# Graph and feed-forward block on one core: where the degrees' column is turned, and when the identity's read is asked for

## The chip, the core and the metric

The kernel runs on one core of a Trainium2 chip. The metric is the device time of one execution in microseconds (us); lower is better. Three executions of the kernel before took 1198.85, 1199.94 and 1200.19 us, a median of 1199.94 us.

## The reference

`x` has 1250 nodes of 1024 features; 20000 edges run from `src` to `dst`. Cut to what matters here:

```python
xn  = layernorm(x)
deg = segment_sum(ones, dst);  deg_inv = 1 / maximum(deg, 1)
def sage(h, Ws, Wn, b):
    mean = segment_sum(h[src], dst) * deg_inv[:, None]
    return h @ Ws + mean @ Wn + b
gnn = sage(relu(sage(xn, Ws0, Wn0, b0)), Ws1, Wn1, b1)
mix = gelu(V(xn @ Wq, xn @ Wk, xn @ Wv) @ Wo + bo)   # linear attention, feature by feature
x   = x + gnn + mix
out = x + ffn(layernorm(x))       # products of quantised codes
```

All the products are made from pairs of f16 parts (a high and a low one), so each product of two f32 matrices is three f16 matmuls.

## The kernel before, in words

Each engine has one program, written out by hand; engines meet at semaphores (`wait_ge`, `then_inc`), and nothing reorders an engine's work. SP (SyncE) asks for nearly all transfers, in the order in which they are written; ACT asks for two at the start.

**Start.** DVE writes `diagonal`, a [128 x 129] tile whose first column is 1. ACT sends it to device memory (L640, semaphore `diag_out`), waits for that (L641), and reads it back with rows of 128 instead of 129, which gives the identity `ident32` (L642, semaphore `ident_in`). PE waits for `ident_in` (L935) before its first transpose. Meanwhile SP asks for ten row tiles of `x` (125 nodes each, `x_all`, L450 to L455) and, between tiles 4 and 5, for the first two slices of weights, of `Wq` and `Wk` (`load(0)`, `load(1)`); behind tile 9 come the edge lists, two more slices (`Wv`, `Ws0`), the biases, and from L479 on the edge keys, which wait for DVE. For each tile DVE makes mean and variance (`x_stats`, L1194), ACT the normed rows (`xn_tile`, L653), PE eight transposes into PSUM (`turn_xn`, L947), ACT the high f16 part (`turned_hi`, L660), DVE the low one (`turned_lo`, L1251). In ACT's own order (L744 to L774) the squares of the two slices of weights (`norms(0, ...)`, L670) and the roots for tiles 2 to 4 (`deviations(1)`, L647) stand ahead of `turned_hi(0)`.

**Products on x.** PE multiplies the normed rows by Wq, Wk, Wv and Ws0 (L970, L983), group of 128 features by group, then by Wo and by Wn0, in halves of 512 columns and tiles of 125 rows (`half_product`, L1053), 40 tiles counted by `i` (0 to 39). `P16` takes the products by Wn0, through ACT (`p_high`, L822) and DVE (`p_low`, L1483). Tile i uses PSUM bank (i + 5) % 6; `mm_free` counts the tiles that DVE has read. GpSimd counts the edges into a matrix of 1250 x 1250 in device memory (L598), which becomes `AT` in f16 (`counts`, L1280).

**Degrees.** Behind tiles 35 and 37 PE sums the columns of `AT` (`degrees`, L991) into banks 6 and 7. DVE takes them behind its own parts of tiles 36 and 38 (L1491 to L1497): maximum with 1 (L1321), and after the second part the reciprocal of 128 x 1250 values (L1497), which sets `dinv_ok`. Only then comes `p_low(39)`. `dinvb` has all nodes' 1/degree in every partition's row.

**Turning the degrees.** For the second aggregation, 1/degree is also wanted as a column per tile of nodes (`dcol`). PE waits for `dinv_ok` (L1071) and makes ten one-row transposes into bank 6 (L1073, `dcol_done`). DVE waits for `dcol_done` (L1507), copies the column (L1508), makes a factor (L1509, L1510) and multiplies `dinvb` by it (L1512).

**First aggregation.** `for g in range(KC)` (L1076) runs over eight groups of 128 features: 60 matmuls each (L1085), of `P16` by `AT`, into PSUM banks 3 to 5 for even g, 0 to 2 for odd g. Groups 0 and 1 wait for `mm_free` to reach 37 and 40, later ones for `ag_free`, DVE's word that the group two before has been read. DVE per group: multiply by `dinvb` (L1524, sets `ag_free`), add the self product (L1527), after ACT's relu (L831) the low part (`h_low`, L1516). Behind it PE goes on to the halves 4 to 7 on `hT` (L1053, L1089 to L1092).

**The rest.** The second aggregation (L1114, L1123) has eight transposes of the next stage between its tiles (L1101); then the feed-forward products (L1151, L1181) and the output.

Of the kernel before, what the change touches and what calls it, by code (L numbers as in the profile page):

```python
# [38 lines left out]
def build(nc, x, src, dst, Ws0, Wn0, b0, Ws1, Wn1, b1, Wq, bq, Wk, bk, Wv, bv, Wo, bo, wgate, wup, wdown, out):  # L39
# [4 lines left out]
    NT = 10  # L44
    TP = N // NT
# [30 lines left out]
    with ctx:  # L76
# [15 lines left out]
        def sb(name, shape, dt, offset=None):  # L92
            if offset is None:
                offset = region(size(shape, dt))
            return nc.alloc_sbuf_tensor_at(name, shape, dt, offset=offset)
# [51 lines left out]
        dinvb = sb("dinvb", [P, N], F32, RG)  # L147
# [27 lines left out]
        ident32 = const("ident32", [P, P], F32)  # L175
# [43 lines left out]
        def bank(b, n=1):  # L219
            return ps[:, b * 512:(b + n) * 512]  # L220

        def acc(par):
            return ps[:, par * 1536:par * 1536 + 1536]
# [7 lines left out]
        def sem(name):  # L231
            return ctx.enter_context(nc.semaphore(name))
# [15 lines left out]
        diag_set, diag_out, ident_in = sem("diag_set"), sem("diag_out"), sem("ident_in")  # L248
# [6 lines left out]
        deg_done, deg_free, dinv_ok, dcol_done = (  # L255
            sem(n) for n in ("deg_done", "deg_free", "dinv_ok", "dcol_done"))
# [92 lines left out]
        for i in range(40, 80):  # L349
            n, t = divmod(i, NT)  # L350
# [29 lines left out]
        def ag1_banks(t, h, n=1):  # L380

            return bank(2 * ((t + 1) % 3) + h, n)
# [4 lines left out]
        def last_bank(n):  # L387
            a, b = LAST_COLS[n]
            return (ag1_banks(NT - 1, n) if n < 2 else ag1_banks(NT - 3, 0))[:, 0:b - a]
# [11 lines left out]
        def w9(j, *of):  # L401

            return w_last[:, of[0], of[1]] if j == NF - 1 else w8[:, j, of[0], of[1]]
# [4 lines left out]
        def load_rows(sp, tile, of, t, done):  # L408

            if t + 1 < NT:  # L410
                sp.dma_start(tile[:, t, :], of[t * TP:t * TP + P, :]).then_inc(done, 32)
            else:
                sp.dma_start(tile[:SPLIT, t, :], of[t * TP:t * TP + SPLIT, :]).then_inc(done, 16)
                sp.dma_start(tile[SPLIT:TP, t, :], of[t * TP + SPLIT:(t + 1) * TP, :]).then_inc(done, 16)
# [7 lines left out]
        def rows(t):  # L422
            return slice(t * TP, (t + 1) * TP)
# [4 lines left out]
        def _(sp):  # L428
            def load(r):

                if r >= NR:
                    worked(sp, r - NR)
                kind, *of = ring[r]
                slot = raw[:, r % NR, :]
                if kind == "chunk":
                    g, i = of
                    view = XW[i].rearrange("(k p) n -> p k n", p=P)[:, :, bass.ts(g, P)]
                    sp.dma_start(slot.rearrange("p (k n) -> p k n", k=KC), view).then_inc(raw_in[r % NR], 16)
                elif kind == "norm":
                    w, k = of  # L440
                    sp.dma_start(slot, MW[w][k * P:(k + 1) * P, :]).then_inc(raw_in[r % NR], 16)
                elif kind == "half":
                    w, h, j = of
                    view = MW[w].rearrange("(k p) n -> p k n", p=P)[:, 2 * j:2 * j + 2, h * HD:(h + 1) * HD]
                    sp.dma_start(slot.rearrange("p (k n) -> p k n", k=2), view).then_inc(raw_in[r % NR], 16)
                else:
                    sp.dma_start(slot.rearrange("p (k n) -> p k n", k=KC), ffn_chunk(of[0])).then_inc(
                        raw_in[r % NR], 16)

            for t in range(5):  # L450
                load_rows(sp, x_all, x, t, x_in[t])
            load(0)
            load(1)
# [480 lines left out]
        def _(pe):  # L934
# [78 lines left out]
            for h in range(2):  # L1013
                mm = pe.transpose(bank(2)[:EP, h * EH:(h + 1) * EH], key_r[:, h, :], ident32[:EH, :EH])
# [12 lines left out]
            for c in range(2, 4 * KC):  # L1027
                product(c)
                g, i = divmod(c, 4)
# [5 lines left out]
            def half_product(n, stationary):  # L1035
                w, part = HALVES[n]
                for t in range(NT):
                    i = 10 * n + t
                    if n == 0 and t < 6:
                        pe.wait_ge(xn_free[0 if (i + 5) % 6 < 3 else 1], 2 * KC)  # L1040
                    elif n == 4 and t < 6:
                        pe.wait_ge(ag_free[0 if t >= 3 else 1], KC // 2)
                    else:
                        pe.wait_ge(mm_free, i - 5)
                    for k in range(KC):
                        if n == 0 and t == 0:
                            pe.wait_ge(v_lo, k + 1)
                        elif n == 4 and t == 0:
                            pe.wait_ge(hl_ok, k + 1)
                        if t == 0 and k % 2 == 0:  # L1050
                            worked(pe, at["half", w, part, k // 2])
                        for ap, wp in ((0, 0), (0, 1), (1, 0)):
                            mm = pe.matmul(half_bank(i), stationary[:, k, ap, t * TP:t * TP + P],  # L1053
                                           hb[:, n % 2, k, wp, :], start=(k == 0 and wp == 0 and ap == 0),
                                           stop=(k == KC - 1 and ap == 1))
                    mm.then_inc(mm_done, 1)
                    if i in W_SUMS:
                        w_sums(W_SUMS[i])
                    if i == DEG_TILE - 1:
                        pe.wait_ge(so_ok, WN1 + 1)  # L1060
                        pe.wait_ge(at_ok, NT + 1)
                        degrees(0, 1024)
                    elif i == DEG_TILE + 1:
                        pe.wait_ge(deg_free, 1)
                        degrees(1024, N)
# [2 lines left out]
            half_product(1, VT)  # L1068
            half_product(2, xnT)
            half_product(3, xnT)  # L1070
            pe.wait_ge(dinv_ok, 1)  # L1071
            for t in range(NT):
                mm = pe.transpose(bank(6)[:TP, t:t + 1], dinvb[0:1, rows(t)], ident32[0:1, 0:1])  # L1073
            mm.then_inc(dcol_done, 1)

            for g in range(KC):  # L1076
                par = (g + 1) % 2
                if g < 2:
                    pe.wait_ge(mm_free, 37 + 3 * g)
                else:  # L1080
                    pe.wait_ge(ag_free[par], g // 2)
                for s in range(NT):
                    for part in range(2):
                        for a, b in NCOLS:
                            mm = pe.matmul(acc(par)[:, a:b], P16[:TP, s, part, bass.ts(g, P)], AT[:TP, s, a:b],  # L1085
                                           start=(s == 0 and part == 0), stop=(s == NT - 1 and part == 1))
                mm.then_inc(ag_done, 1)

            half_product(4, hT)  # L1089
            half_product(5, hT)  # L1090
# [14 lines left out]
            for t in range(NT):  # L1105
# [4 lines left out]
                if t + 1 < NT:  # L1110
                    for h in range(2):
                        for s in range(NT):
                            for part in range(2):
                                mm = pe.matmul(ag1_banks(t, h), AT[:TP, s, t * TP:t * TP + P],  # L1114
                                               P16[:TP, s, part, h * HD:(h + 1) * HD],
                                               start=(s == 0 and part == 0), stop=(s == NT - 1 and part == 1))
                else:
                    for n, (a, b) in enumerate(LAST_COLS):
                        if n == 2:
                            pe.wait_ge(ag1_free, NT - 2)  # L1120
                        for s in range(NT):
                            for part in range(2):
                                mm = pe.matmul(last_bank(n), AT[:TP, s, t * TP:t * TP + P], P16[:TP, s, part, a:b],  # L1123
                                               start=(s == 0 and part == 0), stop=(s == NT - 1 and part == 1))
# [11 lines left out]
            for n, (m, r) in enumerate(UG):  # L1136
# [7 lines left out]
                for b in range(IC):  # L1144
                    if r == 0:
                        pe.wait_ge(w9_in[IC + IC * m + b], 16)
                    for k in range(KC):
                        if n == 0 and b == 0 and k % (KC // 2) == 0:
                            pe.wait_ge(c_lo, k // (KC // 2) + 1)
                        for wp, ap in ((0, 0), (0, 1), (1, 0)):  # L1150
                            mm = pe.matmul(acc(n % 2)[:, b * 512:b * 512 + hi - lo],  # L1151
                                           w9(IC + IC * m + b, wp, slice(k * P, (k + 1) * P)),
                                           codeT[:, k, ap, lo:hi], start=(k == 0 and wp == 0 and ap == 0),
                                           stop=(k == KC - 1 and wp == 1))
# [13 lines left out]
            for r, (a, b) in enumerate(OCOLS):  # L1168
                if r > 0:
                    pe.wait_ge(o_lo, OFIRST + r)  # L1170
                for t in range(a // TP, b // TP):
                    wide = P if b == N or (t + 1) * TP < b else TP
                    for c in range(2):
# [3 lines left out]
                        for k in range(IC):  # L1177
                            if i == 0 and k < OFIRST:
                                pe.wait_ge(o_lo, k + 1)
                            for ap, wp in ((0, 0), (0, 1), (1, 0)):  # L1180
                                mm = pe.matmul(bank(i % 6)[:wide, :], o16[:, k, ap, t * TP:t * TP + wide],  # L1181
                                               w9(k, wp, slice(c * HD, (c + 1) * HD)),
                                               start=(k == 0 and wp == 0 and ap == 0),
                                               stop=(k == IC - 1 and ap == 1))
# [572 lines left out]
```

## Time and profile of the kernel before

| What | Value |
|---|---|
| Median of 3 executions | 1199.94 us |
| Profiled execution, its own time | 1197.6 us |
| Span of its instructions | 1195.8 us |
| Mean granted TensorE clock | 0.996 of 2.4 GHz |
| PE matmul, busy | 1154.0 us (97% of the span) |
| DVE, busy | 670.2 us (56%) |
| ACT, busy | 356.4 us (30%) |
| DMA, mean | 98 GB/s |

The span runs from the first to the last instruction; 1.8 us of the execution lie around it. PE is TensorE's matmuls, PEld its loads of stationary data, DVE VectorE, ACT ScalarE, POOL GpSimd, SP SyncE; a name with a q (SPq) is that engine's queue of requests. "Idle before" is the time in which an engine stood still just ahead of an instruction, with what released it behind the arrow. In the chain of waits each piece is what held up the next piece, so its pieces add up to the span.

### The profile page before, as it was taken

To read this page: it belongs to the slowest core of one execution; us is meant where nothing else is said; L and a number is where in the kernel's file an instruction comes from. 1 tells how busy PE (TensorE), PEld (TensorE's weight loads), DVE (VectorE), ACT (ScalarE), POOL (GpSimd) and SP (SyncE) were. 2 spreads that over 40 slices of the span, in tenths; PEclk is the share of its full clock that TensorE was granted. 3 is DMA by queue.
4 is the path that set the end of the run, shared out by engine and by line. 5 is a ranking of instruction groups with operands and counts; after the bars stand their busy time and mean duration, and the time that the engine had idled before them with its cause. 6 is when DMAs were issued, how large, how long until landed. Compare 5 with 4: busy or idle time off the path is not lost.

```text
span 1195.8 us, 15245 instructions
## 1 busy us (share of the span) xinstructions
PE 1154.0 (97%) x6309; PEld 621.8 (52%) x6309; DVE 670.2 (56%) x1232; ACT 356.4 (30%) x446; POOL 393.2 (33%) x224
## 2 busy tenths in 40 slices
PE   4899999999999999999999899999999999999978
PEld 3455555555555554444444455444444445579934
DVE  7766846749476663334433445646473335582663
ACT  5635243242333422323311022313110012252540
POOL 1266776868778774777300000000000000000000
PEclk9999999999999999999999999999999999999989
DMA  9935526254352439434711134332320070000005
GB/s 261 339 87 154 113 43 153 20 136 77 79 111 20 98 67 332 113 54 139 262 43 39 61 117 149 113 100 88 106 71 36 18 158 1 1 1 2 1 12 160
DMA packets 156151, 117.61 MB, mean 98 GB/s; under 512 B 93401, under 2 KB 132569, under 8 KB 155058
## 3 DMA queue, kind: packets, MB, share of 16 engines
q1 hardware_dynamic: 86744, 103.41, 27.6%
q0 software_dynamic: 69024, 13.07, 8.4%
q8 instruction: 49, 0.80, 0.3%
q10 hardware_dynamic: 314, 0.16, 0.0%
q14 instruction: 20, 0.16, 0.0%
HBM read 90.13 MB, written 21.41 MB: 93 GB/s over the span
## 4 chain that ended last, share of the span: by engine, by line
PE 92%; DVE 4%; issue 1%; ACT 1%; DMA 1%; SPq 0%; POOL 0%; POOLq 0%; ACTq 0%
PE ps L1053 34%; PE ps L983 32%; PE ps L1085 7%; PE ps L1114 6%; PE ps L1151 6%; PE ps L1181 3%; PE ps L970 1%; DMA raw<-in_L_mix_Wk_dram 1%; PE ps L1123 1%; DVE dinvb L1497 1%; PE ps L1101 1%; DVE key_b L1263 0%; PE ps L991 0%; DVE stats L1197 0%; ACT xs L653 0%
## 5 line engine op out<-in xcount | busy, mean ns | idle before, releaser
L598 POOL DMA_INDIRECT at_scratch<-copies,cell x160 | 345.6, 2160 | 161.1 <-DMA at_scratch<-copies,cell 89.1
L983 PE MATMUL ps<-xnT,whl 128*128 128x512 f16 (+1 forms) x2160 | 381.8, 339 | 0.0
L983 PEld LDWEIGHTS ps<-xnT,whl 128*128 128x128 f16 x2160 | 210.6, 98 | 168.9
L1053 PE MATMUL ps<-hb,hT 128*128 128x512 f16 x960 | 207.7, 379 | 1.3 <-DVE hT L1516 1.3
L1053 PEld LDWEIGHTS ps<-hb,hT 128*128 128x128 f16 x960 | 94.0, 98 | 114.4 <-DVE hT L1516 1.8
L579 POOL PARTITION_ALL_REDUCE ag_fw<-am_fw x9 | 3.2, 354 | 312.7 <-DVE am_fw L1399 312.7
L1053 PE MATMUL ps<-hb,VT 128*128 128x512 f16 x480 | 103.9, 379 | 1.5 <-ACT S_b L740 1.5
L1053 PE MATMUL ps<-hb,xnT 128*128 128x512 f16 x480 | 104.2, 379 | 0.0
L1085 PE MATMUL ps<-AT,P 125*128 125x512 f16 (+1 forms) x480 | 86.1, 343 | 0.0
L1114 PE MATMUL ps<-P,AT 125*128 125x512 f16 x360 | 79.0, 379 | 0.0
L1483 DVE SCALAR_TENSOR_TENSOR P<-ps,P 125x512 f16<-125x512 f32 x40 | 27.5, 689 | 91.9 <-ACT P L822 91.8
L1053 PEld LDWEIGHTS ps<-hb,VT 128*128 128x128 f16 x480 | 46.9, 98 | 58.0 <-ACT S_b L740 1.9
L1053 PEld LDWEIGHTS ps<-hb,xnT 128*128 128x128 f16 x480 | 47.0, 98 | 56.1
L575 POOL PARTITION_ALL_REDUCE ag<-am x5 | 1.8, 351 | 218.3 <-DVE am L1610 218.3
L1151 PE MATMUL ps<-codeT,w 128*128 128x250 f16 x600 | 65.2, 269 | 2.1 <-DVE codeT L1636 2.1
L1085 PEld LDWEIGHTS ps<-AT,P 125*128 125x128 f16 x480 | 47.1, 99 | 38.6 <-issue 1.6
L1151 PEld LDWEIGHTS ps<-codeT,w 128*128 128x128 f16 x600 | 57.8, 96 | 8.9 <-issue 1.8
L822 ACT ACTIVATE P<-ps 125x512 f16<-125x512 f32 x40 | 23.7, 594 | 116.4 <-PE ps L1053 116.3
L1114 PEld LDWEIGHTS ps<-P,AT 125*128 125x128 f16 x360 | 35.2, 98 | 40.9
L688 ACT ACTIVATE whl<-raw,sc 128x1024 f16<-128x1024 f32 x32 | 35.0, 1138 | 69.1 <-DVE inv L1233 69.1
L1245 DVE SCALAR_TENSOR_TENSOR whl<-raw,sc,whl 128x1024 f16<-128x1024 f32 x32 | 40.3, 1281 | 15.8 <-ACT whl L688 15.8
L1460 DVE SCALAR_TENSOR_TENSOR ps<-ps,sv,bo_b 125x512 f32<-125x512 f32 x20 | 15.0, 757 | 52.5 <-PE ps L1053 41.0
(231 smaller groups left out, 1204.6 us busy)
## 6 DMA issues: line engine op xcount, KB each, us to landing
raw<-in_L_gnn_W_neigh_dram SPq DMA_DIRECT2D x32, 512.0 KB, 4.5
raw<-in_L_gnn_W_self_dram SPq DMA_DIRECT2D x24, 512.0 KB, 5.2
key_b<-key_scratch SPq DMA_DIRECT2D x8, 1250.0 KB, 7.0
raw<-in_L_mix_Wo_dram SPq DMA_DIRECT2D x16, 512.0 KB, 3.6
parts<-at_scratch POOLq DMA_DIRECT2D x20, 312.5 KB, 4.7
at_scratch<-zeros POOLq DMA_DIRECT2D x6, 1020.0 KB, 17.8
x_all<-in_x_dram SPq DMA_DIRECT2D x9, 512.0 KB
x_acc<-in_x_dram SPq DMA_DIRECT2D x9, 512.0 KB
```

Source lines behind the costliest of these rows:

```text
L598: pool.indirect_dma_start(out=at_scr[c % 2][:, :], out_offset=bass.IndirectOffsetOnAxis(ap=cell[:, c:c + 1], axis=0), in_=copies[:, c:c + ...
L688: act.activation(whl[:, i, 0, :, :].rearrange("p k n -> p (k n)"), raw[:, at["chunk", g, i] % NR, :], ACT.Copy, scale=sc[:, g % 2, i:i + 1 ...
L822: act.activation(P16[:TP, t, 0, h * HD:(h + 1) * HD], half_bank(i)[:TP, :], ACT.Copy, scale=scale).then_inc(p_hi, 1)
L983: mm = pe.matmul(acc_of(c)[:, a:b], whl[:, i, wp, k, :], xnT[:, k, ap, a:b], start=(k == 0 and wp == 0 and ap == 0), stop=(k == KC - 1 and ...
L1053: mm = pe.matmul(half_bank(i), stationary[:, k, ap, t * TP:t * TP + P], hb[:, n % 2, k, wp, :], start=(k == 0 and wp == 0 and ap == 0), st ...
L1085: mm = pe.matmul(acc(par)[:, a:b], P16[:TP, s, part, bass.ts(g, P)], AT[:TP, s, a:b], start=(s == 0 and part == 0), stop=(s == NT - 1 and ...
L1114: mm = pe.matmul(ag1_banks(t, h), AT[:TP, s, t * TP:t * TP + P], P16[:TP, s, part, h * HD:(h + 1) * HD], start=(s == 0 and part == 0), sto ...
L1151: mm = pe.matmul(acc(n % 2)[:, b * 512:b * 512 + hi - lo], w9(IC + IC * m + b, wp, slice(k * P, (k + 1) * P)), codeT[:, k, ap, lo:hi], sta ...
L1181: mm = pe.matmul(bank(i % 6)[:wide, :], o16[:, k, ap, t * TP:t * TP + wide], w9(k, wp, slice(c * HD, (c + 1) * HD)), start=(k == 0 and wp ...
L1245: dve.scalar_tensor_tensor(whl[:, i, 1, :, :].rearrange("p k n -> p (k n)"), raw[:, at["chunk", g, i] % NR, :], sc[:, g % 2, i:i + 1], whl ...
L1460: dve.scalar_tensor_tensor(b, b, sv[:TP, INV_O:INV_O + 1], bo_b[:TP, h * HD:(h + 1) * HD], ALU.mult, ALU.add).then_inc(m1_ok, 1)
L1483: dve.scalar_tensor_tensor(P16[:TP, t, 1, at_p], half_bank(i)[:TP, :], scale, P16[:TP, t, 0, at_p], ALU.mult, ALU.subtract).then_inc(mm_fr ...
```

## The change

Two edits. SP waits for `diag_out` before it asks for tile 3 of `x`, so that ACT's read of the identity, which waits for the same semaphore, is not behind tiles 3 and 4 of `x` and the first weights. PE makes the ten transposes of the degrees (with the wait for `dinv_ok`) behind the matmuls of the aggregation's group 0 and no longer ahead of them. DVE's program is unchanged.

```diff
             for t in range(5):
+                if t == 3:
+
+                    sp.wait_ge(diag_out, 16)
                 load_rows(sp, x_all, x, t, x_in[t])
             load(0)
             load(1)
@@
             half_product(3, xnT)
-            pe.wait_ge(dinv_ok, 1)
-            for t in range(NT):
-                mm = pe.transpose(bank(6)[:TP, t:t + 1], dinvb[0:1, rows(t)], ident32[0:1, 0:1])
-            mm.then_inc(dcol_done, 1)
-
             for g in range(KC):
                 par = (g + 1) % 2
                 if g < 2:
@@
                 mm.then_inc(ag_done, 1)
+                if g == 0:
+                    pe.wait_ge(dinv_ok, 1)
+                    for t in range(NT):
+                        mm = pe.transpose(bank(6)[:TP, t:t + 1], dinvb[0:1, rows(t)], ident32[0:1, 0:1])
+                    mm.then_inc(dcol_done, 1)
```

## Rows read from the trace of the kernel before

**Rows 1.** The page: chain that ended last, shares of the span by line.

```profile
PE ps L1053 34%; PE ps L983 32%; PE ps L1085 7%; PE ps L1114 6%; PE ps L1151 6%; PE ps L1181 3%; PE ps L970 1%; DMA raw<-in_L_mix_Wk_dram 1%; PE ps L1123 1%; DVE dinvb L1497 1%; PE ps L1101 1%; DVE key_b L1263 0%; PE ps L991 0%; DVE stats L1197 0%; ACT xs L653 0%
```

**Rows 2.** Chain of waits, 640 to 765: start us, us, what.

```profile
648.14 5.20 PE ps L1053 x24
...
655.02 7.98 DVE dinvb L1497
...
663.04 1.53 PE ps L1073 x10
664.56 86.00 PE ps L1085 x480
```

**Rows 3.** Timeline, 630 to 775: start us, us, engine, line, operation [idle before].

```profile
642.66 0.69 DVE L1483 SCALAR_TENSOR_TENSOR P<-ps,P 125x512 f16<-125x512 f32 x1 [8.81 <-ACT P L822]
...
647.98 10.53 PE L1053 MATMUL ps<-hb,xnT 128*128 128x512 f16 x48
...
663.04 1.53 PE L1073 MATMUL ps<-ident,dinvb 1*125 1x1 f32 x10 [4.53 <-DVE dinvb L1497]
...
676.73 0.10 DVE L1522 MEMSET hT<- 128x48 uint32 x1 [10.43 <-PE ps L1085]
...
687.19 1.46 DVE L1524 TENSOR_TENSOR Tg<-ps,dinvb 128x1250 f32<-128x1250 f32 x1 [4.67 <-PE ps L1085]
...
697.76 1.46 DVE L1524 TENSOR_TENSOR Tg<-ps,dinvb 128x1250 f32<-128x1250 f32 x1 [4.78 <-PE ps L1085]
...
750.59 1.46 DVE L1524 TENSOR_TENSOR Tg<-ps,dinvb 128x1250 f32<-128x1250 f32 x1 [3.76 <-PE ps L1085]
```

**Rows 4.** Busy time by stretch, 653 to 677; PEclk is the granted clock.

```profile
653.30:658.50 5.20, 5.20 (x25) 2.16 (x22) 4.47 (x3) 0.60 (x1) 0.00 (x0) 1.00 0.00 0
664.50:666.00 1.50, 1.50 (x6) 0.63 (x6) 1.31 (x7) 0.00 (x0) 0.00 (x0) 0.50 0.00 0
666.00:668.00 2.00, 2.00 (x10) 0.96 (x9) 0.30 (x1) 0.00 (x0) 0.00 (x0) 0.68 0.00 0
668.00:670.00 2.00, 2.00 (x14) 1.05 (x12) 0.00 (x0) 0.00 (x0) 0.00 (x0) 1.00 0.00 0
```

**Rows 5.** Chain of waits, whole span: transposes between the second aggregation's tiles.

```profile
976.68 0.85 PE ps L1101 x8
977.54 8.63 PE ps L1114 x40
```

**Rows 6.** Timeline, 663 to 667: DVE behind the transposes.

```profile
662.90 0.63 DVE L1483 SCALAR_TENSOR_TENSOR P<-ps,P 125x512 f16<-125x512 f32 x1
...
664.79 0.16 DVE L1508 COPY dcol<-ps 125x10 f32<-125x10 f32 x1
...
665.43 0.87 DVE L1512 TENSOR_SCALAR dinvb<-dinvb,sv 128x1250 f32<-128x1250 f32 x1
```

**Rows 7.** Requests to landing in the first 40 us (last column: median us).

```profile
raw<-in_L_mix_Wk_dram SPq DMA_DIRECT2D x1, 512.0 KB, 10.2
diag_scratch<-diagonal ACTq DMA_DIRECT2D x1, 64.5 KB, 4.6
ident<-diag_scratch ACTq DMA_DIRECT2D x1, 64.0 KB, 4.9
```

**Rows 8.** Timeline, 0 to 40: the start.

```profile
5.77 0.33 ACTq L642 DMA_DIRECT2D ident<-diag_scratch  x1
...
10.75 3.59 PE L947 MATMUL ps<-ident,xs 125*128 125x125 f32 x16 [10.75 <-DMA ident<-diag_scratch]
...
14.08 1.06 ACT L670 ACTIVATE squared<-raw 128x1024 f16<-128x1024 f32 x1 [0.67 <-DMA raw<-in_L_mix_Wk_dram]
...
15.37 0.99 ACT L660 ACTIVATE xnT<-ps 128x1000 f16<-128x1000 f32 x1
```

**Rows 9.** Busy time by stretch, DMA: last two columns are share and GB/s.

```profile
0.00:6.70 6.70, 0.00 (x0) 0.00 (x0) 2.27 (x7) 0.57 (x1) 0.92 (x11) 1.00 0.70 244
0.73:1.73 1.00, 0.00 (x0) 0.00 (x0) 0.23 (x2) 0.00 (x0) 0.72 (x7) 1.00 0.00 0
3.30:9.00 5.70, 0.00 (x0) 0.00 (x0) 3.94 (x12) 1.59 (x3) 0.00 (x0) 1.00 1.04 408
```

**Rows 10.** Chain of waits, the start: from the weights' landing on.

```profile
2.12 0.04 issue
...
3.80 10.20 DMA raw<-in_L_mix_Wk_dram
...
52.62 9.84 PE ps L970 x72
```

## The prediction

> **What bounds the kernel now.** I read the page's chain first. The lines that hold it are PE's matmuls nearly throughout [rows 1]; two lines that are no matmul carry about one per cent each, the landing of the first slice of Wk and the reciprocal of the degrees, L1497. Those are the two places of the change. Time taken out of PE's line anywhere behind the start is therefore time taken off the end, unless something else comes to wait.
>
> Next the chain near the aggregation [rows 2]: PE's tile 38, then DVE's reciprocal for 7.98 us, the ten transposes for 1.53, then the 480 matmuls of the aggregation. The timeline shows how much of this PE really loses [rows 3]. Tile 39 runs beside the reciprocal and ends at 647.98 + 10.53 = 658.51; PE then stands still for 4.53 us until 663.04. The third view is the clock [rows 4]: 1.00 up to 658.5 (2.4 GHz); behind the stop 0.50 (1.2 GHz) from 664.5 to 666, 0.68 on average until 668, then 1.00 again. So group 0 of the aggregation pays for the stop a second time.
>
> At the start I read the chain again [rows 10]: it goes through Wk's landing at 14.0, then through ACT and DVE in turn, to PE's product at 52.6. The identity is not in it.
>
> **Part one: the transposes behind group 0.** Group 0 asks only for `mm_free` 37, that is DVE's part of tile 36, done at 642.66 + 0.69 = 643.35 [rows 3]. So it starts where tile 39 ends, at 658.51.
> - A group at full clock: from DVE's take-up of group 1 to that of group 2, 697.76 - 687.19 = 10.57; over the seven intervals from 676.73 to 750.59, 73.86 / 7 = 10.55 [rows 3]. Group 0 before, from 664.56 to 676.73 [rows 2, 3], took 12.17, so 1.62 more, the half clock.
> - Group 0 after: 658.51 + 10.55 = 669.06. The reciprocal is ready at 663, six us earlier, so PE doesn't wait for `dinv_ok`.
> - The transposes: 1.53 at half clock is the upper bound [rows 2]. The lower one is the eight transposes of the later stage at full clock, 0.85 us, or 0.106 each [rows 5]: ten take 1.06. I take 1.25, between the two, as these are of another shape. End: 670.31.
> - Seven more groups, 73.86: 744.17, against 750.59. Gain 6.4 us, which is 4.53 of stop, 1.62 of clock and 0.28 of faster transposes. Bounds 6.1 to 6.6 from the transposes alone.
>
> What waits now? DVE's work behind `dcol_done` runs from 664.79 to 665.43 + 0.87 = 666.30, so 1.5 us [rows 6]. It used to lie under group 0; now it stands between group 0's end and its reading. DVE is done with it at 671.8 and frees group 0's banks, after one more multiplication of 1.46 [rows 3], at 673.3. Group 2 wants them at 670.31 + 10.55 = 680.9. Cover 7.6 us, so cost 0; were it gone, each us more of DVE's work would cost one. Group 1 wants `mm_free` 40, given behind the reciprocal at 663.5 [rows 6]: there seven us early. From group 1 on, each wait has the distances it had before. The last thing PE waits for, the low part of group 7, moves with group 7.
>
> At the clock, the row shows that eight transposes of 0.85 us between two tiles of matmuls cost nothing beyond themselves, the 40 matmuls behind them taking 8.63 us as a full-speed piece [rows 5]. The Trainium skill, "TensorE: Matmul & The Clock Gate", section "Part 4: PE-mode transpose", says that a transpose does not count as busy the way a matmul does. By that rule the ten might act as a stop; the sum would lose up to the 1.62 us that a real stop has cost. I go by the row.
>
> **Part two: SP's wait at tile 3.** ACT's request for the identity leaves at 5.77, when `diag_out` is there [rows 8]; SP's wait ends at the same event. Up to then SP has asked for tiles 0 to 2 (the third request ends by 2.12 [rows 10]); so tile 3 is asked for at about 5.8 in place of 2.2, and tile 4, Wq and Wk follow, each later than before. Everything behind them on SP's queue, tiles 5 to 9, edges, weights, biases, is held too.
> - What hides it: the DMA engines work off a backlog at 408 GB/s [rows 9]. Three tiles (512 KB each, as Wk [rows 7]) and the diagonal are 1.64 MB; by 6.70 the core had moved 244 x 6.7 = 1.63 MB [rows 9]. So there is work until 6.7. Tile 3's first bytes come some 1.0 us after the request, as at the beginning (nothing moves from 0.73 to 1.73 [rows 9]), at 6.8. The hole is nominally 0.1 us, more if the rate takes time to rise, as it does at the start. The identity's 64 KB, 0.16 us at that rate, fall into it and leave Wk's way. Bounds: 0 (all covered) and 3.6 (Wk late by the whole pause). I take 0.4, near the covered end, because the backlog is in the rows.
> - What it brings: the identity, now landing 4.9 us after its request with much traffic ahead [rows 7], may land two us or so sooner. PE's first transposes would start before 10.75 by some tenths, as ACT's normed tile is there about then. But their reader, ACT at L660, starts at 15.37, behind the squares of Wk, which begin at 14.08 with its landing [rows 8]. The transposes end at 14.3, already before it. Gain 0.
> - Wk's delay passes on one to one, as the chain has no slack between 14.0 and 52.6 [rows 10].
>
> **Sum.** -6.4 + 0.4 = -6.0 us. The profiled execution's own 1197.6 becomes 1191.6. It lies 2.3 under the median of the three; on the median's scale, 1199.94 - 6.0 = 1193.9.
>
> **Rivals.**
> 1. *The pause at the start is not covered.* If `diag_out` or the refilling of the queue is slow, Wk lands up to 3.6 late: 1199.9 - 6.4 + 3.6 = 1197.1. For it: the rate rises slowly at the beginning, and Wk is in the chain [rows 10]. Against: the backlog until 6.7. Chance 0.12, counting a delay over 1.5.
> 2. *The clock falls in the transposes*: the ten count as a stop and group 1 begins at half clock, as group 0 did behind the real one, +1.62 [rows 2, 3], so 1195.5. Against: the transposes that left the next tile at full speed [rows 5]. Chance 0.05. This is what the rule of the Trainium skill named above would give.
> 3. *The start gets faster.* Wk lands sooner, because the identity's traffic and later tiles no longer mix into it, or PE's earlier transposes matter: up to 1 us, 1192.5. For it: PE's stop of 10.75 us is the longest named at the start [rows 8]. Against: ACT's order. Chance 0.15.
> 4. *Slower than before.* The place is again SP's wait: it costs one us for each us that `diag_out` comes behind about 5.7. The other part's gain is eaten from 5.7 + 6.4 = 12.1 on. The diagonal took 4.6 to land with more traffic beside it [rows 7]; with less it should not take 11. At 15, the time would be 1202.8. Chance 0.02.
> 5. *The move of the transposes brings nothing*, because PE waits elsewhere in the aggregation: only if DVE's extra 1.5 us met less than that of cover, and it has 7.6. Time 1200.3. Chance 0.04.
>
> The forecast itself, 1193 to 1195.4, has 0.62.
>
> **Numbers.** A measurement of this kernel tells 0.2% from no change, 2.4 us, so faster means below 1197.5. The forecast and rivals 2 and 3 are all faster, and nearly all of rival 1. Faster 0.91, same 0.06, slower 0.03. For eight in ten I reach from rival 3's end, less the spread of some tenths of a median (1198.85 to 1200.19 among three), to just under rival 1's end: 1191.8 to 1196.6.
>
> **What would show it.** In the changed kernel: no idle time of PE before L1085's first matmul, which starts about 658 plus what the start lost; L1073 behind it, with no wait for `dinv_ok`, taking 1.1 to 1.5 us; clock 1.00 throughout; the first DVE L1508 some 6 us later than before and L1524 at full pace, with no wait of PE for DVE at groups 2 to 7. At the start: tile 3 asked for at 5.8, the identity landing before 10, Wk at 14.0 to 15.0, and the product L970 at 52.6 to 53.6 still last. Wrong would be: Wk at 16 or later, a PE wait for `ag_free`, or a clock of 0.5 in group 1.

## The result

The changed kernel took 1192.75 us in the median of four executions (1192.35 to 1194.39), against 1199.70 before (four executions, 1198.85 to 1200.19). The ratio is 0.9945, 95% interval 0.993 to 0.996: 6.6 us faster by the ratio, between 4.8 and 8.4. Forecast were 1193.9, range 1191.8 to 1196.6. The profiled execution of after took 1193.08 (span 1191.3), that of before 1197.6: those two differ by 4.5 us only. That is 2 us less than the ratio says, and most of the experiments go to this difference.

The chain of waits of after, 635 to 765 us (start, us, what), beside [rows 2]:

```profile
649.88 10.36 PE ps L1056 x48
660.25 10.57 PE ps L1083 x60
670.81 1.18 PE ps L1089 x10
671.99 74.09 PE ps L1083 x420
```

The reciprocal has left the chain. Tiles 38 and 39 (10.36 us for both) are followed without a stop by group 0, in 10.57 us, then the transposes in 1.18, then seven groups in 74.09. The busy time by stretch has the clock (PEclk, third from the end) at 1.00 throughout, where [rows 4] fell to 0.50:

```profile
658.00:670.00 12.00, 12.00 (x67) 6.36 (x66) 8.34 (x10) 0.60 (x1) 0.00 (x0) 1.00 0.17 53
670.00:672.00 2.00, 2.00 (x16) 1.53 (x15) 0.00 (x0) 0.00 (x0) 0.00 (x0) 1.00 0.00 0
```

DVE in the timeline of after, beside [rows 6]: its work behind the transposes now begins at 672.03, and group 0 is read from 673.64 on. Group 1 is taken at its proper time, 682.70.

```profile
672.03 0.17 DVE L1511 COPY dcol<-ps 125x10 f32<-125x10 f32 x1 [5.41 <-PE ps L1089]
...
672.68 0.87 DVE L1515 TENSOR_SCALAR dinvb<-dinvb,sv 128x1250 f32<-128x1250 f32 x1
...
673.64 1.41 DVE L1527 TENSOR_TENSOR Tg<-ps,dinvb 128x1250 f32<-128x1250 f32 x1
...
682.70 1.46 DVE L1527 TENSOR_TENSOR Tg<-ps,dinvb 128x1250 f32<-128x1250 f32 x1 [3.32 <-PE ps L1083]
```

The start, in the timeline of after, beside [rows 8]:

```profile
5.54 0.36 ACTq L645 DMA_DIRECT2D ident<-diag_scratch  x1
...
6.86 0.58 SPq L438 DMA_DIRECT2D raw<-in_L_mix_Wk_dram  x1
...
10.81 3.60 PE L950 MATMUL ps<-ident,xs 125*128 125x125 f32 x16 [10.81 <-DMA ident<-diag_scratch]
...
15.86 1.06 ACT L673 ACTIVATE squared<-raw 128x1024 f16<-128x1024 f32 x1 [0.69 <-DMA raw<-in_L_mix_Wk_dram]
```

The squares of Wk begin 1.78 us later than before, and the identity is there no sooner: PE's first transposes start at 10.81 against 10.75. The DMA traffic by stretch (last two columns: share, GB/s) shows the hole, in this profile of after:

```profile
6.00:7.00 1.00, 0.00 (x0) 0.00 (x0) 0.93 (x5) 1.00 (x1) 0.00 (x0) 1.00 0.64 262
7.00:8.00 1.00, 0.00 (x0) 0.00 (x0) 0.93 (x4) 0.21 (x1) 0.00 (x0) 1.00 0.45 133
8.00:9.00 1.00, 0.00 (x0) 0.00 (x0) 0.66 (x5) 0.24 (x2) 0.00 (x0) 1.00 0.98 372
```

PE's product of 72 matmuls, the first piece of the chain behind the start, begins at 54.37 against 52.62 in [rows 10], 1.75 later. Shifted back by that, the aggregation ends 6.2 us sooner (746.08 - 1.75 = 744.33 against 664.56 + 86.00 = 750.56 [rows 2]): 4.53 of stop and 1.7 of clock. So the two profiles say: -6.2 + 1.75 = -4.5. Do they stand for the usual execution?

### The profile page after: what moved, and what is told of

It reads as the page before. It is cut to its first block, busy times and chain, and to the rows that moved or that the text cites. A ratio compares the mean times of both kernels' runs of the same rounds, so it can differ in the third digit from the quotient of the medians.

```text
span 1191.3 us, 15245 instructions
## 1 busy us (share of the span) xinstructions
PE 1155.2 (97%) x6309; PEld 622.5 (52%) x6309; DVE 669.0 (56%) x1232; ACT 356.3 (30%) x446; POOL 389.6 (33%) x224
## 4 chain that ended last, share of the span: by engine, by line
PE 94%; DVE 3%; issue 1%; DMA 1%; ACT 1%; SPq 0%; POOL 0%; POOLq 0%; ACTq 0%
PE ps L1056 34%; PE ps L986 32%; PE ps L1083 7%; PE ps L1117 7%; PE ps L1154 6%; PE ps L1184 3%; PE ps L973 2%; DMA raw<-in_L_mix_Wk_dram 1%; PE ps L1126 1%; PE ps L1104 1%; PE ps L994 0%; DVE stats L1200 0%; PE ps L950 0%; DVE xnT L1254 0%; DMA diag_scratch<-diagonal 0%
## 5 line engine op out<-in xcount | busy, mean ns | idle before, releaser
L601 POOL DMA_INDIRECT at_scratch<-copies,cell x160 | 341.9, 2137 | 164.5 <-DMA at_scratch<-copies,cell 95.6
```

Source lines behind the costliest of these rows:

```text
L601: pool.indirect_dma_start(out=at_scr[c % 2][:, :], out_offset=bass.IndirectOffsetOnAxis(ap=cell[:, c:c + 1], axis=0), in_=copies[:, c:c + ...
```

## The experiments

Each was run beside the kernel before on the same chip: runs 1 to 4 on one chip (median of before 1199.29), 5 to 8 on a second (1199.51), 9 to 11 on a third (1198.95). Where two experiments are compared, it is by their medians. "The wait" is SP's wait for `diag_out`, "the turning" the move of the ten transposes, and "the product of 72 matmuls" PE's first product behind the start, L970 of the kernel before. Line numbers in the profiles move by a few lines with each edit.

**1. Both edits.** 

> Both edits, as changed. The profiles of before and after differ by 4.5 us of span, the medians of the timed executions by 6.95. Theory 1 (the turning of the degrees gains 6.2 us, SP's wait costs 1.7 us by Wk's later landing): 4.5 us faster than before, ratio 0.9962. Theory 2 (SP's wait costs nothing, or gains, in a usual execution): 6.2 us faster or more, ratio 0.9948 or less.

Measured: 1192.12 us, ratio 0.9944 (0.993 to 0.9957), 7.2 under the 1199.29.

**2. SP's wait alone.**

```diff
             for t in range(5):
+                if t == 3:
+                    sp.wait_ge(diag_out, 16)
                 load_rows(sp, x_all, x, t, x_in[t])
```

> SP's wait ahead of tile 3 alone. Theory 1: 1.7 us slower than before, ratio 1.0014, Wk landing at 15.8 us. Theory 2: within 0.5 us of before, or faster. In both the aggregation is as before: PE stands still 4.5 us ahead of the ten transposes and group 0 takes 12.2 us.

Measured: 1199.69 us, ratio 1.0002 (0.9993 to 1.0011): 0.4 us slower in the median; the interval, 0.8 us faster to 1.3 slower, excludes 1.7. The squares of Wk begin at 14.89. The aggregation holds the surprise, in its chain of waits and its busy time by stretch:

```profile
655.76 7.98 DVE dinvb L1500
...
663.78 2.25 PE ps L1076 x10
666.04 86.28 PE ps L1088 x480
```

```profile
664.00:666.00 2.00, 2.00 (x11) 1.98 (x12) 1.34 (x9) 0.00 (x0) 0.00 (x0) 0.50 0.00 0
666.00:668.00 2.00, 2.00 (x7) 0.84 (x7) 1.42 (x4) 0.00 (x0) 0.00 (x0) 0.50 0.00 0
668.00:670.00 2.00, 2.00 (x10) 0.96 (x8) 0.00 (x0) 0.00 (x0) 0.00 (x0) 0.67 0.00 0
```

The stop is 4.53 us, as before, but what follows it is dearer: the transposes take 2.25 us in place of 1.53, and the clock is back at 1.00 only after 668, where in [rows 4] it was by then. This stretch of code is the same as in the kernel before. From tile 39's end at 659.25 to the end of the aggregation it takes 93.07 us, and 92.05 in the profile of before (658.51 to 750.56): the clock's part is 2.7 us here, in place of 1.7.

**3. The turning alone.** The second edit without the first.

> The ten transposes behind group 0 alone, no wait on SP. Theory 1: 6.2 us faster than before, ratio 0.9948, and 1.7 us faster than with both edits; Wk lands at 14.0 us. Theory 2: no faster than with both edits.

Measured: 1191.81 us, ratio 0.9937 (0.9924 to 0.9951), 7.5 under 1199.29 and 0.3 under both edits. Its chain has group 0 in 10.57 us, the transposes in 1.18 and seven groups in 74.09, as after. So by the medians the turning gains more than the 6.2 of the two profiles. This run's own interval, 5.9 to 9.1 us, does not exclude 6.2; that runs 6 and 10, which also have the turning without the wait, lie 7.7 and 7.2 under before speaks against it as well. The wait's 1.7 is excluded by run 2. Theory 1 falls in its sizes.

**4. SP's wait ahead of tile 1.** Both edits, `t == 3` made `t == 1`.

> Both edits, but SP waits ahead of tile 1, so only tile 0 is asked for before the diagonal has landed. Theory 1 (the wait costs what it leaves the DMA engines without work): two tiles less of backlog, 2.6 us more at 400 GB/s, so Wk lands at about 18 us and the time is 2.5 us over that with both edits. Does the identity limit PE's first transposes? If it does, they start well before 10.8 us here, since nothing is ahead of its read; if they start at 10.8 or later with tile 0's normed rows, it does not.

Measured: 1194.60 us, 2.5 slower than both edits, the number that theory 1 gave; PE's product of 72 matmuls begins at 55.70 against 53.30 in run 1, 2.4 later. The path is not theory 1's. The squares of Wk begin at 16.79 and not at 18, and ACT does not wait for Wk's landing there. Tile 1's statistics begin only at 8.61, the scales of tiles 0 and 1 are made together, and one small step of DVE among them takes 2.31 us, in place of 0.17 in the profile of after. It ends at 13.11, with GpSimd's memset of `zeros`, which ends at 13.08:

```profile
9.59 3.49 POOL L574 MEMSET zeros<- 128x4080 f16 x1
...
10.80 2.31 DVE L1209 TENSOR_SCALAR ln<-ln 125x2 f32<-125x2 f32 x1
```

That step stands in the chain of waits of this run, and only behind it come the normed tile 0, at 14.6, and PE's start, at 14.73. So how much of the 2.5 us is the longer hole, and how much these 2.1 us of meeting the memset, is not shown; that the number fits is no evidence for the hole alone. The identity, with one tile ahead of it, landed 3.9 us after its request at 4.91, at 8.8. The question on the identity gets no answer here, as the normed tile moved too.

**5. Filler matmuls in the stop.** The order of before; PE is kept busy while it waits for the reciprocal, by a helper that the kernel before already uses in other places (L937).

```diff
+            pe.wait_ge(mm_free, 38)
+            keep_busy(20, bank(0), ones16[:, :], xnT[:, 0, 0, 0:512])
             pe.wait_ge(dinv_ok, 1)
```

> The kernel before, with the transposes ahead of group 0 as they were, and 20 filler matmuls of 512 columns (4.3 us, results unused) ahead of the wait for the reciprocal. The stop of 4.5 us stays as time, but PE is busy in it. Theory 1 (the move gains 4.5 us of stop and, apart from that, whatever the half clock behind it costs): clock 1.00 through group 0, transposes 1.2 us, group 0 10.57 us; the time falls by the clock's part alone, 1.9 us against the profiled execution of before and about 2.9 in the median of the timed ones. Theory 2 (the clock's part is small in a usual execution and something else made the medians differ by more than the profiles): under 1 us.

Measured: 1196.26 us, ratio 0.9976 (0.9966 to 0.9985): 3.25 us under 1199.51 in the median, 2.9 by the ratio (1.8 to 4.1), with PE no further in its work when the reciprocal is there. The chain and the clock of the filler's kernel:

```profile
663.42 1.25 PE ps L1075 x10
664.66 84.66 PE ps L1087 x480
```

```profile
663.00:665.00 2.00, 1.78 (x13) 1.37 (x13) 1.79 (x9) 0.00 (x0) 0.00 (x0) 1.00 0.00 0
665.00:667.00 2.00, 2.00 (x13) 1.13 (x12) 1.53 (x6) 0.00 (x0) 0.00 (x0) 1.00 0.00 0
```

This is the clock's part by itself: 3.25 us by the medians, where the two profiles gave 1.7 and the prediction 1.9. With the stop of 4.53 it makes 7.8, near the 7.5 of run 3. No profile shows as much as 3.25: from the product of 72 matmuls to the end of the aggregation the profile of before takes 1.6 us more than that of this run, and that of run 2 2.6 more. Theory 2 of this run's expectation falls.

**6. Another order at the start,** on the kernel of run 3: ACT takes the turned tile 0 ahead of the squares of Wk, and DVE its low part ahead of the scales.

```diff
             norms(0, (0,))
+            turned_hi(0)
             norms(0, (1,))
             deviations(1)
-            turned_hi(0)
-            xn_tile(2)
             turned_hi(1)
+            xn_tile(2)
...
-            x_scale(1)
             turned_lo(0)
-            prepare_scale(0)
+            x_scale(1)
             turned_lo(1)
+            prepare_scale(0)
```

> The turning behind group 0, no wait on SP, and at the start ACT takes the turned tile 0 ahead of the squares of Wk, tile 1 ahead of the normed tile 2; DVE takes turned tile 0 ahead of the scales. If the start hangs on ACT's order behind Wk's landing, PE's product behind the start begins earlier by 0.5 to 1.5 us than with the turning alone, and so does the end. If DVE's own work binds from there on, no change within 0.3 us.

Measured: 1191.82 us, against 1191.81 for run 3: nothing gained. The product of 72 matmuls begins at 53.06, against 52.88. The turned tile 0 is taken 1.8 us earlier (13.86 against 15.68), and the stage behind it does not follow.

**7. The turning behind group 1.** On the kernel of run 3, `g == 0` made `g == 1`.

> The ten transposes behind group 1 in place of group 0, no wait on SP. The cover of DVE's work behind them is then used up: with the transposes ending 22.3 us behind group 0's start, DVE frees group 0's banks 3.0 us later, and group 2 waits for that: 3.0 us slower than with the turning behind group 0. If the cover is not what the sums of the prediction say, the stop is larger or missing.

Measured: 1196.94 us, ratio 0.9982 (0.9973 to 0.9991), 5.1 slower than run 3, not 3.0. The timeline has the stop as foretold, 3.11 us:

```profile
684.55 15.81 PE L1080 MATMUL ps<-AT,P 125*128 125x512 f16 x79 [3.11 <-DVE Tg L1524]
```

The rest is the clock again, in the busy time by stretch: 0.61 and 0.54 of full speed from 685 to 689, then 1.00. The six groups behind the stop take 65.27 us in the chain, against 6 x 10.57 = 63.4 us at the full clock, so 1.9 more. Stop and clock make 5.0 of the 5.1. The ten transposes stand directly ahead of the stop here (1.19 us from 680.26), so PE goes 4.3 us without a matmul; whether they have a share in the fall of the clock was not separated.

```profile
685.00:687.00 2.00, 2.00 (x9) 1.03 (x8) 1.04 (x1) 0.92 (x1) 0.00 (x0) 0.61 0.00 0
687.00:689.00 2.00, 2.00 (x8) 0.85 (x6) 1.64 (x2) 1.36 (x3) 0.00 (x0) 0.54 0.92 265
```

**8. SP's wait ahead of tile 4.** Both edits, `t == 3` made `t == 4`.

> Both edits, but SP waits ahead of tile 4, so the DMA engines have four tiles of backlog, which last to about 8 us. Theory 1 (the wait costs the time that the engines stand without work): no hole, Wk lands at 14.0 to 14.5 us, and the time is that with the turning alone, 0.3 us under both edits. Theory 3 (the wait costs by the order in which transfers are asked for): Wk lands later than 15 us here too.

Measured: 1191.98 us, ratio 0.9941 (0.9927 to 0.9954), within 0.2 of the turning alone. No hole: 430 and 406 GB/s where after had 262 and 133. The squares of Wk begin at 14.62, and the product at 52.82.

```profile
6.00:7.00 1.00, 0.00 (x0) 0.00 (x0) 0.93 (x5) 0.79 (x1) 0.00 (x0) 1.00 1.05 430
7.00:8.00 1.00, 0.00 (x0) 0.00 (x0) 0.93 (x4) 0.50 (x1) 0.00 (x0) 1.00 1.00 406
```

With one tile more of backlog the hole is gone, as theory 1 has it. The identity, asked for at 5.82, meets PE at 11.27 and brings nothing.

**9. The low part of tile 9 sooner,** on the kernel of run 3: an attempt at a faster start.

```diff
                 for q in range(CPP):
+                    if p == 0 and q == 15:
+                        turned_lo(NT - 1)
...
             cells(0)
-            turned_lo(NT - 1)
```

> The turning behind group 0, no wait on SP, and DVE takes the low part of tile 9 of x (1.2 us) behind 15 of the first 20 key comparisons in place of behind all of them and the five small steps that follow. In the traces PE stands still for up to 1.5 us at 50.7 to 52.2 for that low part, or not at all where its matmuls before it ran at the half clock. Expected: 0.3 to 1.4 us faster than the turning alone, PE's product (the one of 72 matmuls at 52.9) starting 0.3 to 1.3 us sooner; the tail of the comparisons delays only GpSimd, whose edge counting has over 20 us of slack before its first reader. If the keys or the scales behind it become the bound, nothing is gained.

Measured: 1191.66 us, ratio 0.9939 (0.9926 to 0.9953), against 1191.77 for the turning alone beside it: not shown to be faster. Its five executions run from 1190.22 to 1193.62. In the profile the 12 matmuls ahead of tile 9 took 4.26 us in place of the 2.76 of the profile of before, so that there was no stop to save. PE in the timeline, first in this run:

```profile
44.41 4.26 PE L970 MATMUL ps<-xnT,whl 128*128 128x512 f16 x12 [2.33 <-DVE xnT L1251]
```

And in the profile of before, where the clock stayed at 1.00 and a second stop, for tile 9, followed:

```profile
44.52 2.76 PE L970 MATMUL ps<-xnT,whl 128*128 128x512 f16 x12 [2.33 <-DVE xnT L1251]
...
52.24 0.38 PE L958 MATMUL ps<-nq,ones 128*128 128x4 f32 x2 [1.51 <-DVE xnT L1251]
```

From these 12 matmuls to the product of 72 it is 7.89 us in run 9 and 8.10 or 8.11 in the profiles of all the other kernels, at either clock.

**10 and 11. The turning alone and both edits, again.**

> The turning alone again, on the same chip and beside both edits, to size SP's wait: if the hole in the DMA traffic costs what the start's traces show, 0.4 to 1.0 us faster than both edits; if the first pair's 0.3 us was chance, no difference.

> Both edits again, as partner of the turning alone: 0.4 to 1.0 us slower than it if the wait costs by its hole. Against before: 6.5 to 7.5 us faster.

Measured: 1191.77 and 1192.47 us, 0.7 apart. The ten executions of each kind from runs 1, 3, 10 and 11 have medians of 1192.37 and 1191.79: the wait costs 0.6 us. The two kinds overlap (1192.02 to 1194.48 against 1191.26 to 1192.87), so its sign is likely rather than certain. The begin of the product of 72 matmuls shows why two profiles can't size it. With the wait ahead of tile 3 it was 54.37, 53.30, 53.37 and 53.75 (after, runs 1, 2 and 11); without it, 52.62, 52.88, 53.01, 53.24 and 54.17 (before, runs 3, 5, 7 and 10). The means are 53.7 and 53.2, 0.5 apart, and one kernel alone varies by over 1 us.

## Why the prediction was right, and which term was off

**The total** was 6.0 us, measured 6.6 by the ratio (7.2 and 6.5 by the medians of runs 1 and 11). Both terms had the right sign and place. With the terms as the experiments measured them, the sum would have been 4.5 + 3.25 - 0.6 = 7.2.

**The stop** of 4.53 us went as forecast. Group 0 starts where tile 39 ends and finds the reciprocal ready; no other wait of PE took its place.

**The clock term was mis-sized.** The step was "Group 0 before took 12.17, so 1.62 more, the half clock", with 0.28 for faster transposes, 1.9 together. In the chains of the two profiles it is 1.7: 0.35 for the transposes (1.53 against 1.18) and 1.34 for the groups (86.00 against 10.57 + 74.09). Filler matmuls in the stop gain 3.25. The profile of before was a lucky one in this: its granted clock was 0.996, and its time, 1197.6, lies under all the other executions of before shown with it. Of the 44 executions of before that ran beside the experiments the median is 1199.3, and the three fastest (1197.64, 1197.88, 1197.93) are the three whose clock was 0.996; the others had 0.989 to 0.994. Run 2's profile, of an execution at 0.991, has a longer stretch at 0.50, worth 2.7 us. The prediction noted that the profiled execution was 2.3 us under the median, and carried that difference over to the changed kernel as if it had nothing to do with the change. That was the error: by the medians 3.25 - 1.9, some 1.3 us of it, belonged to the very stop that the change removes (0.8 by run 2's profile). What decides how long the half clock lasts behind a stop was not tested.

**The transposes** took 1.18 us, forecast 1.25 between bounds of 1.06 and 1.53; the upper bound was itself no bound, as run 2 shows 2.25 at the half clock throughout. Group 1 behind them runs at clock 1.00, so rival 2 is out. The Trainium skill, "TensorE: Matmul & The Clock Gate", section "Part 4: PE-mode transpose", says that a transpose doesn't count as busy the way a matmul does. Here 1.2 us of transposes between two groups had no effect on the clock in any of the profiles of the turning behind group 0. A longer row of transposes between matmuls, which could tell more of that rule, no run here has.

**DVE's cover** of 7.6 us was right. Moving the turning one group further used it up and left a stop of 3.11, forecast at 3.0. The price of that stop was 5.1 and not 3.0, since I had again left the clock out of the sum.

**SP's wait** was put at 0.4 us, near the covered end, and costs 0.6 by the pooled medians. In the profile of after the cost was 1.75. The forecast was "the hole is nominally 0.1 us"; in the profiles the rate falls to 133 to 214 GB/s between 7 and 8 us, so the hole is nearer 1 us long (0.7 to 1.0 us as an estimate, from the rates of the four profiles between 6 and 8 us against 408 GB/s). The squares of Wk begin at 15.86, 14.82, 14.89 and 15.29 in the four profiles with the wait ahead of tile 3, and at 14.08, 14.39, 14.40, 14.29 and 14.20 in the five without it (before and runs 3, 5, 7 and 10): 0.9 us later in the mean. The delay passes on one to one, as forecast: from the squares to the product of 72 matmuls it is 38.46 to 38.51 us in the four with the wait, and 38.54, 38.49 and 38.61 in before and runs 3 and 5. But it is 38.95 in run 7 and 39.97 in run 10, which is why the mean shows only half. There the small step of DVE that run 4 held up, 0.17 us when undisturbed, takes 0.97 and 1.50 us, and it ends within 0.03 us of the end of GpSimd's memset of `zeros` (so it does in all six profiles in which it is longer than 0.17); in run 10 the first 24 matmuls behind it also fall to the half clock, 7.04 us in place of 5.35. With the wait ahead of tile 3 the memset begins sooner (11.4 to 12.0 us against 12.5 to 13.8) and the step later, and they do not meet. In these profiles the wait so has a small gain beside its cost. Why the memset's begin moves, and why DVE's other steps are not held up beside it, is not shown, and two profiles do not say how often it happens. Run 8 (backlog one tile longer, no hole) bears out that the hole is what delays Wk; run 4 does not by itself, for the reason given there. Rival 1, over 1.5 us, is not the usual case, and rival 3, a faster start, did not come.

**The identity** was forecast to land two us or so sooner and to bring nothing. It landed (request plus time to landing) at 10.7, 9.9, 9.9 and 10.4 us with the wait (after, runs 1, 2 and 11), and at 10.7, 12.1, 11.1, 11.3 and 11.1 without (before, runs 3, 5, 7 and 10): 1.0 us sooner in the mean. Even so no time came of it. (In run 8, where the wait cost nothing, it landed at 11.2, no sooner than without the wait.) ACT's order behind Wk stands ahead of the reader, and in run 6, which loosened that order, the next stage did not follow. A request with little ahead of it on the queues still took 4.6 to 5.2 us, and 3.9 with a single tile ahead (run 4). Why it takes so long was not settled.

## What to carry to other kernels

A stop of the tensor engine is worth more than its length: its price includes the matmuls behind it at half clock, here 3.25 us on top of 4.5, and 1.9 on top of 3.1. Where another stop stands close behind, it can cost nothing: at this kernel's start the half clock behind a stop of 2.33 us only filled the 1.51 us of the next one. Size that part from several executions; an execution whose granted clock is above the usual shows it too small. And where the stop cannot be moved, filler matmuls in it win back the clock's part. Work that only a later stage needs (here a column of ten values) is best put behind one unit of work that does not need it, after counting what its reader may then delay: one group was free, two cost 5 us. A wait on the queue of transfers is free only while the requests ahead of it keep the DMA engines busy: here behind four tiles of 512 KB, and no longer behind three.

## What was not expected

- The same code, the same stop of 4.53 us: half clock until about 667 in one profile (transposes 1.53 us), until about 669 in another (2.25 us).
- A stop of 3.11 us, with ten one-row transposes just ahead of it, was enough to bring the clock from 1.00 down to 0.61 and 0.54 in the mean for some 4 us (run 7), and the filler of 20 matmuls that nobody reads made the kernel 3.25 us faster.
- A DVE step on 125 x 2 or 125 x 3 values, 0.17 us elsewhere, took up to 2.31 us and ended with a memset of GpSimd (run 4, and shorter in five other profiles).
- A stop of 2.33 us at the start (ahead of the 12 matmuls before tile 9) is followed by 2.76 us for them in five profiles (before, runs 1, 2, 6 and 7) and by 4.2 to 4.5 at the half clock in the other eight. This is no part of the start's spread: the product of 72 matmuls comes 8.1 us behind their begin either way.
- A read of 64 KB took 3.9 to 6.0 us to land, 4.6 or more of it even behind three tiles only.
